# A new order of work in a fused attention and expert kernel: score pairs, half values and half down projections

## The chip, the cores and the metric

The kernel runs on one core of a Trainium2 chip. The metric is the device time of one launch in microseconds (us), lower is better; for the kernel before, three runs are given, and the median counts.

## The reference

The input is 64 sequences of 128 tokens and width 128, with a context of 120 tokens of width 96 for each. What is computed is one gated layer:

```
x = x + tanh(g_xattn) * cross_attention(layernorm(x), ctx)      # 16 heads of 8, biases, softmax over 120 keys
x = x + tanh(g_ffn)   * ffn_block(layernorm(x))
ffn_block(x):
    h = rms(x) ; q = rms(heads(h wq)) ; k = rms(heads(h wk)) ; v = heads(h wv)
    x = x + causal_softmax(q k / sqrt(8)) v wo                  # the first 32 columns of the product set to 0
    xf = rms(x) ; probs = softmax(xf gate) ; the best 2 of 4 experts, weights normalised
    moe = w0 gelu(xf up) down + w1 silu(xf w1)(xf w2) down + w2 four-layer gelu net + w3 three-layer gelu net
    return x + moe                                              # the first 32 columns of moe set to 0
```

All four experts are computed for every token, in fp32.

## The kernel before, in words

The 64 sequences are worked in 16 groups of 4. The work on a group is cut into five parts: N (layer norm of the input, transposes, the projections q, k, v of the cross attention), A (cross attention), B (norm and projections of the self attention), D (self attention, router, the first layers of the experts) and M (the later layers of the experts and the output). They are a software pipeline: in one step of the loop, part N works on group t+1, A on t, B on t-1, D on t-2 and M on t-3. Twelve steps form the loop (`LOOP`, t = 3 to 14); ahead of it stand four ramp steps (`first_group` to `fourth_group`) and behind it four tail steps, each with an order of its own (`RAMP`, `TAIL`; `last_queries`, t = 15, is made from the loop's order without N).

The order is written out by hand, as one list of uses for a step, `SCHEDULE = self_attention() + second_experts() + cross_attention() + first_experts()` (lines 112 to 160). Every engine walks through that list in its `step` function and issues its own part of each use, so one list sets the order on PE, ACT (ScalarE), DVE (VectorE), POOL (GpSimd) and SP's DMA queue alike. Engines run in order; a wait of one use holds all that stands behind it on that engine.

The eight PSUM banks belong to rings: four banks `w0` to `w3`, two banks `s2a`, `s2b` (the scores and, as ring "f", expert layers), one `pv` and one `t`. `bank_of_each_use` hands out the banks of a ring in turn, in the order of the list. A matmul waits until the former use of its bank has been read (`drained`), so the n-th use of the ring "w" waits for the reader of the use four places earlier.

The uses that the change and the prediction's steps touch:

- `exact(part, b, first)`: a pair of exact scores (s2), two fp32 matmuls of 512 columns for four heads each, into ps_s2a and ps_s2b (line 1342). ACT takes exponentials of each into `probs` (line 951). For D, POOL then masks both tiles of a pair in one select (lines 817 and 818), behind a tick.
- `values(part, b)`: four groups of eight small matmuls with `probs` (line 1363), into ps_pv; two batches share ps_pv, and the last of them is copied by ACT (oT, line 955). For D, each waits for the mask of its pair.
- `estimate(part, b)`: rough scores in bf16 for all 16 heads (lines 1302 and 1306) into all four w banks. DVE takes the negated maxima (line 1092), four reductions.
- mT: the transposed maxima (line 1315), copied by ACT and sent by SP's DMA into qd, on which the first exact scores of the next block wait. mH and mL are the same in halves, in the ramp.
- down e: the down projection of expert e, 16 matmuls (line 1389) into a w bank; DVE adds the four results into ym (line 1121).
- oT, nT, wo: transposes of the values (DVE: reciprocal line 1131, scaling line 1133), transposes back (ACT's copy, line 958) and the output projection (line 1376, DVE lines 1143 and 1148), all through the bank t.
- B: hT (transposes of hb, which DVE makes in line 1032), qk (line 1274, ACT's copy line 896), squares (POOL, line 829), sums (DVE, line 1067), root (ACT, line 905), scale (DVE, lines 1071 and 1073), qT and kT (transposes).
- B init: DVE writes x2 (line 1042). It waits for `xf_ready`, that is until ACT's `D norm` (four activations into xf, line 881) has read the old x2.
- D xfT: transposes of xf (line 1225) into a w bank; logits; then e1_w1, e1_w2, e2_l1, e3_down, e0_up, the first layers of the experts (line 1408).

In the loop's order the w ring is used like this (number of the use in the step): estimate A0 6 to 9, A1 10 to 13, down 0 14, A2 15 to 18; in the cross block v 27, down 2 28, xT 29, estimate B0 30 to 33, B1 34 to 37, down 3 38, xfT 39, B2 40 to 43, logits 44, e1_w1 45.

Of the kernel before, what the change touches and what calls it, by code (L numbers as in the profile page):

```python
# [31 lines left out]
P = 128  # L32
# [8 lines left out]
UP = P - KEEP  # L41
G = 4
# [4 lines left out]
NT = H // HT  # L47
VW = HD + 1
PACK = 2
# [42 lines left out]
def values(part, b):  # L92

    return [(part, "pv", (b, c), "pv" if b % 2 and c == NT - 1 else None) for c in range(NT)]
# [12 lines left out]
def down(e):  # L107

    return fill("M", "down", e, "w")
# [12 lines left out]


def second_experts():

    return (fill("M", "e2_l2", 0) + one("D", "wo", 0, "t") + one("B", "scale", 0, None) + fill("M", "e2_l2", 1)
            + estimate("A", 3) + values("D", 3) + fill("M", "e3_up", 0) + one("D", "oT", 1, "t") + fill("M", "e3_up", 1)
            + one("N", "stats", 0, None)
            + one("D", "nT", 1, "t") + one("A", "mT") + fill("M", "e2_l3", 0) + one("N", "norm", 0, None) + one("D", "wo", 1, "t")
            + one("D", "out", 0, None) + one("B", "qT") + one("B", "kT") + one("D", "squares", 0, None)  # L130
            + fill("M", "e2_l3", 1, "w"))
# [71 lines left out]
def fourth_group():  # L203
# [3 lines left out]
            + one("D", "wo", 0, "t") + estimate("A", 3) + values("D", 3) + one("D", "oT", 1, "t") + one("A", "mT")  # L207
            + one("B", "scale", 0, None) + one("D", "nT", 1, "t") + one("N", "stats", 0, None) + one("D", "wo", 1, "t")
# [16 lines left out]
def last_self_keys():  # L225
# [11 lines left out]
            + fill("M", "down", 2, "pv") + estimate("B", 2) + one("D", "norm", 2, None) + one("B", "init", 0, None) + one("B", "copy", 0, None)  # L237
            + one("D", "xfT", 0, "t") + fill("M", "down", 3, "pv") + one("M", "store", 0, None) + one("B", "v", 0, "f") + one("D", "logits", 0, "t")
# [22 lines left out]
def last_experts():  # L261

    return (fill("M", "down", 1, "t") + fill("M", "e2_l2", 0) + fill("M", "e2_l2", 1) + down(0) + fill("M", "e2_l3", 0) + fill("M", "e2_l3", 1)
            + fill("M", "e3_up", 0, "w") + fill("M", "e3_up", 1, "w") + down(2) + down(3) + one("M", "store", 0, None))
# [156 lines left out]
def build(nc, x, ctxT, weights, vcols, rows, out):  # L421
    ctx = ExitStack()
    with ctx:
# [782 lines left out]
        def _(pe):  # L1206
# [21 lines left out]
            def step(st):  # L1228
                for part, work, index in st.works:
# [149 lines left out]
                    elif work == "fill" and index[0] == "down":  # L1379
                        h = DOWN_OF[index[1]]  # L1380
                        if index[1] in (0, 1):
                            sources = st.settled(*(("f",) if st.parts == "M" and index[1] == 1 else ("w", "f")))
                        else:
                            sources = st.drains([("M", "fill", (h, k)) for k in range(2)])
                        for b, v in merged(sources, st.drains([], key)):
                            pe.wait_ge(drained[b], v)
                        for b in range(G):
# [70 lines left out]
```

## Time and profile before

| what | value |
|---|---|
| three runs | 1071.01, 1071.3, 1073.17 us; median 1071.3 |
| the profiled execution, its own time | 1074.17 us |
| span of the profiled execution | 1072.5 us |
| PE matmuls, busy | 1009.0 us, 94% of the span |
| VectorE, busy | 788.7 us, 74% |
| ScalarE, busy | 736.5 us, 69% |
| GpSimd, busy | 338.1 us, 32% |
| mean granted TensorE clock | 0.982 |
| chain of waits that ended last | PE 65%, DVE 14%, ACT 11%, issue 6%, DMA 2% |

The profiled execution is 1.7 us longer than its span, and 2.9 us above the median of the runs. The clock is given as a share of 2.4 GHz: 1.00 is 2.4 GHz and 0.50 is 1.2 GHz. PE's busy time counts matmuls whose ends are modelled, so two of them can overlap in the records; the distance between two starts is the surer reading of what work costs. An engine's idle time only matters where PE, or what PE waits for, stands behind it.

### The profile page before, as it was taken

The numbers are of one execution on the slowest core, as the hardware profiler recorded it, in microseconds if no ns is written. First come the engines' busy times: TensorE is split into PE (matmuls) and PEld (weight loads), VectorE is DVE, ScalarE is ACT, GpSimd is POOL, SyncE is SP. The second block draws the span as 40 slices with busy tenths as digits, with TensorE's granted clock in tenths as the row PEclk, the third lists the DMA queues.
The fourth block names the chain that finished last, engine by engine and source line by source line (L and its number), as shares of the span: only waits on it lengthen the run. The fifth ranks groups of instructions, "written<-read, shape, count | busy, mean of one in ns | idle before, by whom it ended". The sixth has DMA issues, their size and how long they took to land.

```text
span 1072.5 us, 26205 instructions
## 1 busy us (share of the span) xinstructions
PE 1009.0 (94%) x8649; PEld 627.7 (59%) x8649; DVE 788.7 (74%) x2172; ACT 736.5 (69%) x1334; POOL 338.1 (32%) x463
## 2 busy tenths in 40 slices
PE   6768799999999999999999999999999999999898
PEld 5445556556565655656565565656556565656565
DVE  8546878777877877787787778778777877774723
ACT  6465767676777767677776767777676777767453
POOL 5613424141422414142241414224141422404130
PEclk9868999999999999999999999999999999999999
DMA  7424432233342224334222443422244342221200
GB/s 233 127 72 158 133 104 89 88 130 128 115 134 96 87 88 130 128 115 135 97 86 88 130 128 115 135 96 87 88 130 128 115 135 96 82 79 49 83 1 20
DMA packets 77317, 114.28 MB, mean 107 GB/s; under 512 B 7776, under 2 KB 40160, under 8 KB 77152
## 3 DMA queue, kind: packets, MB, share of 16 engines
q1 hardware_dynamic: 76800, 111.53, 32.1%
q10 hardware_dynamic: 480, 2.26, 0.6%
q8 instruction: 23, 0.38, 0.1%
q14 instruction: 14, 0.11, 0.0%
HBM read 58.97 MB, written 53.74 MB: 105 GB/s over the span
## 4 chain that ended last, share of the span: by engine, by line
PE 65%; DVE 14%; ACT 11%; issue 6%; DMA 2%; SPq 1%; POOL 0%; ACTq 0%; DVEq 0%; POOLq 0%
PE ps_pv L1363 9%; PE ps_w L1389 9%; PE ps_s2a L1342 7%; PE ps_s2b L1342 5%; PE ps_s2a L1401 5%; PE ps_s2b L1408 4%; ACT probs L951 4%; PE ps_t L1225 4%; PE ps_w L1408 3%; PE ps_w L1274 3%; DVE mpadA L1092 3%; PE ps_t L1376 2%; PE ps_w L1225 2%; PE ps_w L1306 2%; PE ps_w L1302 2%
## 5 line engine op out<-in xcount | busy, mean ns | idle before, releaser
L951 ACT ACTIVATE probs<-ps_s2a 120x512 f32<-120x512 f32 (+1 forms) x256 | 153.4, 599 | 76.6 <-PE ps_s2a L1342 68.5
L1092 DVE TENSOR_REDUCE mpadB<-ps_w 128x4 f32<-128x512 f32 x240 | 148.8, 683 | 22.7 <-PE ps_w L1306 22.7
L1092 DVE TENSOR_REDUCE mpadA<-ps_w 128x4 f32<-128x480 f32 x224 | 131.5, 650 | 38.1 <-PE ps_w L1306 38.1
L951 ACT ACTIVATE probs<-ps_s2b 120x512 f32<-120x512 f32 (+1 forms) x256 | 153.5, 599 | 0.0
L818 POOL TENSOR_SCALAR_AFFINE_SELECT probs<-probs 128x1024 f32<-128x1024 f32 x128 | 139.8, 1092 | 0.0
L1389 PE MATMUL ps_w<-W,hid 128*128 128x96 f32 x976 | 121.3, 278 | 1.0 <-DVE split_k L985 0.9
L1389 PEld LDWEIGHTS ps_w<-W,hid 128*128 128x128 f32 x976 | 113.8, 192 | 10.4 <-issue 4.9
L786 POOL TENSOR_TENSOR rB<-vrB,neg_half 128x4 f32<-128x4 f32 x16 | 16.1, 1008 | 204.5 <-DVE veB L978 204.5
L1342 PE MATMUL ps_s2a<-qdA,kstA 128*120 128x512 f32 x128 | 70.2, 548 | 9.2 <-DMA qdA<-scratch_Aq 4.8
L1401 PE MATMUL ps_s2a<-hid,W 128*128 128x512 f32 x152 | 74.4, 604 | 0.0
L1121 DVE SCALAR_TENSOR_TENSOR ym<-ps_w,gates,ym 128x96 f32<-128x96 f32 x184 | 45.7, 311 | 38.6 <-PE ps_w L1389 38.6
L955 ACT ACTIVATE oT<-ps_pv 128x512 f32<-128x512 f32 x64 | 38.3, 598 | 50.9 <-PE ps_pv L1363 50.9
L1342 PE MATMUL ps_s2a<-qdB,kstB 128*128 128x512 f32 x128 | 64.6, 505 | 7.6 <-ACT probs L951 2.1
L1363 PE MATMUL ps_pv<-probs,VA 120*18 120x128 f32 x2048 | 71.2, 282 | 0.0
L947 ACT ACTIVATE hid<-ps_s2a 128x512 f32<-128x512 f32 x73 | 43.7, 599 | 40.0 <-PE ps_s2a L1401 30.9
L1363 PE MATMUL ps_pv<-probs,VB 128*18 128x128 f32 x2048 | 68.4, 274 | 0.0
L1363 PEld LDWEIGHTS ps_pv<-probs,VA 120*18 120x18 f32 x2048 | 51.9, 100 | 24.2 <-issue 22.9
L817 POOL TENSOR_TENSOR tick<-one 128x1 f32<-128x1 f32 x128 | 24.9, 194 | 117.5 <-ACT probs L951 113.2
L1363 PEld LDWEIGHTS ps_pv<-probs,VB 128*18 128x18 f32 x2048 | 50.5, 97 | 17.2 <-issue 16.9
L958 ACT ACTIVATE onT<-ps_t 128x256 f32<-128x256 f32 x64 | 24.5, 384 | 51.6 <-PE ps_t L1225 51.6
L1342 PE MATMUL ps_s2b<-qdA,kstA 128*120 128x512 f32 x128 | 59.3, 463 | 0.0
L825 POOL TENSOR_TENSOR ym<-yb,one 128x128 f32<-128x128 f32 x16 | 6.4, 398 | 166.2 <-DMA out_x<-ym 166.2
(279 smaller groups left out, 2170.3 us busy)
## 6 DMA issues: line engine op xcount, KB each, us to landing
scratch_Aq<-split_q SPq DMA_DIRECT2D x48, 256.0 KB, 2.4
qdA<-scratch_Aq SPq DMA_DIRECT2D x64, 192.0 KB
scratch_Bq<-split_q SPq DMA_DIRECT2D x48, 256.0 KB, 2.4
scratch_Bk<-split_k SPq DMA_DIRECT2D x48, 256.0 KB, 2.9
qdB<-scratch_Bq SPq DMA_DIRECT2D x64, 192.0 KB
kstB<-scratch_Bk SPq DMA_DIRECT2D x64, 192.0 KB
scratch_Ak<-split_k SPq DMA_DIRECT2D x48, 240.0 KB, 2.3
kstA<-scratch_Ak SPq DMA_DIRECT2D x64, 180.0 KB
```

Source lines behind the costliest of these rows:

```text
L818: pool.affine_select(out=tile, in_=tile, compare_op=ALU.is_ge, fill=0.0, base=0, pattern=[[0, 2 * HT], [1, P]], channel_multiplier=-1).the ...
L947: nc.scalar.activation(hid[:, HID_AT[index[0]] + index[1], :], bank[:], ACT.Gelu).then_inc(done, 1)
L951: nc.scalar.activation(probs[0:k, slot_of(part, *index), :], bank[0:k, :], ACT.Exp, scale=SCALE if part == "A" else 1.0).then_inc(done, 1)
L955: nc.scalar.activation(oT[:], bank[:], ACT.Copy).then_inc(done, 1)
L1092: nc.vector.tensor_reduce(pair[:, :, c, b % 2] if halves else mneg[p][:, :, c, b], bank[:, 0:HT * k].rearrange("p (h k) -> p h k", h=HT), ...
L1121: ins = nc.vector.scalar_tensor_tensor(out=ym[:, b, KEEP:P], in0=bank[:, b * UP:(b + 1) * UP], scalar=gates[:, b, e:e + 1], in1=y[:, b, KE ...
L1225: ins = nc.tensor.transpose(psum[st.bank[key]][:, b * P:(b + 1) * P], of(b), identf[:])
L1342: mm(o, kst[p][:, c, b * k:(b + 1) * k], qd[p][:, :, c, b * P:(b + 1) * P], start=True, stop=True).then_inc(done, 1)
L1363: ins = mm(psum[st.bank[last]][32 * j:32 * j + VS, at:at + P], VB[p][0:k, first:first + VS], probs[0:k, slot_of(part, b, c), j * P:(j + 1) ...
L1389: ins = mm(bank[:, b * UP:(b + 1) * UP], hid[:, HID_AT[h] + k, b * P:(b + 1) * P], w[f"down{index[1]}"][:, k * UP:(k + 1) * UP], start=k = ...
L1401: ins = mm(bank[:], w[name][:, k * HID + c * P:k * HID + (c + 1) * P], hid[:, HID_AT[h] + k, :], start=k == 0, stop=k == chunks[-1])
L1408: mm(bank[:], w[name][:, c * P:(c + 1) * P], xfT[:], start=True, stop=True).then_inc(done, 1)
```

## The change

The order of the loop's step and of two ramp steps is laid out anew; what is computed, and the number of matmuls, stay.

- `values` can be issued in halves (`early_values` for the first two groups of heads, `late_values` for the others).
- Down 0 and down 3 are issued in two halves in the loop's order: `head` (batches 0 and 1, no semaphore at its end) and `rest`, both into the same bank. The waits stand in the head. Where no other work stands between them (`down(e)`), the instructions are those of before.
- Self block: estimates no longer stand inside the two pairs of a batch. Between pairs stand halves of values, two qk, or a half of down 0. Estimates A1 and A2 move later (A2 into `second_experts`, with `scale` between A2 and A3), down 0 ahead of A1.
- `second_experts`: nT of the second pair of batches behind e2_l3 0; qT and kT ahead of wo 1, of D's out and of its squares.
- Cross block: down 3 moves from behind values A1 to behind xT, in halves; the output's store with it. Estimates B0, B1, B2 stand behind the second pair of batches 1, 2 and 3; D's norm and B's init now ahead of B0, and xfT behind A2's first pair.
- Third ramp step (t = 1): hT first, qk directly behind the first batch's pairs, mL behind them. Fourth ramp step: as the loop's self block.

In the new order the w ring's uses are: A0 6 to 9, down 0 10, A1 11 to 14, A2 15 to 18; v 27, down 2 28, xT 29, down 3 30, B0 31 to 34, xfT 35, B1 36 to 39, logits 40, B2 41 to 44, e1_w1 45.

```diff
+def early_values(part, b):
+    return values(part, b, 0, PACK)
+def late_values(part, b):
+    return values(part, b, PACK, NT)
...
 def self_attention():
-    return (one("N", "load", 0, None) + one("N", "ctx", 0, None) + exact("D", 0, 0) + one("B", "hT") + down(1) + exact("D", 0, 2)
-            + one("B", "qk", 0) + one("B", "qk", 1) + one("B", "qk", 2) + one("B", "qk", 3)
-            + exact("D", 1, 0) + estimate("A", 0) + exact("D", 1, 2)
-            + one("B", "squares", 0, None) + values("D", 0)
-            + exact("D", 2, 0) + estimate("A", 1) + exact("D", 2, 2)
-            + values("D", 1) + one("B", "sums", 0, None) + down(0)
-            + exact("D", 3, 0) + one("D", "oT", 0, "t") + estimate("A", 2) + exact("D", 3, 2)
-            + one("A", "base", 0, None) + values("D", 2) + one("D", "nT", 0, "t") + one("B", "root", 0, None))
+    return (one("N", "load", 0, None) + one("N", "ctx", 0, None) + exact("D", 0, 0) + one("B", "hT") + down(1)
+            + exact("D", 0, 2) + one("B", "qk", 0) + one("B", "qk", 1) + early_values("D", 0)
+            + exact("D", 1, 0) + one("B", "qk", 2) + one("B", "qk", 3) + late_values("D", 0)
+            + exact("D", 1, 2) + one("B", "squares", 0, None) + estimate("A", 0) + early_values("D", 1)
+            + exact("D", 2, 0) + head(0) + late_values("D", 1)
+            + exact("D", 2, 2) + one("B", "sums", 0, None) + rest(0) + one("D", "oT", 0, "t")
+            + exact("D", 3, 0) + early_values("D", 2) + estimate("A", 1) + one("D", "nT", 0, "t") + late_values("D", 2)
+            + exact("D", 3, 2) + one("A", "base", 0, None) + one("B", "root", 0, None))
 def second_experts():
...
+    return (one("D", "wo", 0, "t") + early_values("D", 3) + estimate("A", 2) + fill("M", "e2_l2", 0) + one("B", "scale", 0, None)
+            + late_values("D", 3) + fill("M", "e2_l2", 1) + estimate("A", 3) + fill("M", "e3_up", 0) + one("D", "oT", 1, "t")
+            + fill("M", "e3_up", 1) + one("N", "stats", 0, None) + one("A", "mT") + fill("M", "e2_l3", 0) + one("D", "nT", 1, "t")
+            + one("N", "norm", 0, None) + one("B", "qT") + one("B", "kT") + one("D", "wo", 1, "t")
+            + one("D", "out", 0, None) + one("D", "squares", 0, None) + fill("M", "e2_l3", 1, "w"))
 def cross_attention():
-    return (exact("A", 0, 0) + one("B", "v") + down(2) + exact("A", 0, 2) + one("N", "xT")
-            + exact("A", 1, 0) + estimate("B", 0) + exact("A", 1, 2)
-            + one("D", "norm", 0, None) + one("B", "init", 0, None) + one("B", "copy", 0, None) + values("A", 0)
-            + exact("A", 2, 0) + estimate("B", 1) + exact("A", 2, 2)
-            + values("A", 1) + down(3) + one("M", "store", 0, None) + one("D", "xfT")
-            + exact("A", 3, 0) + one("A", "oT", 0, "t") + estimate("B", 2) + exact("A", 3, 2)
-            + values("A", 2) + one("D", "logits") + one("A", "nT", 0, "t"))
+    return (exact("A", 0, 0) + one("B", "v") + down(2) + exact("A", 0, 2) + one("N", "xT") + head(3)
+            + exact("A", 1, 0) + rest(3) + one("M", "store", 0, None)
+            + exact("A", 1, 2) + values("A", 0) + one("D", "norm", 0, None) + one("B", "init", 0, None) + one("B", "copy", 0, None)
+            + estimate("B", 0)
+            + exact("A", 2, 0) + one("D", "xfT") + values("A", 1)
+            + exact("A", 2, 2) + one("A", "oT", 0, "t") + estimate("B", 1)
+            + exact("A", 3, 0) + values("A", 2) + one("D", "logits")
+            + exact("A", 3, 2) + estimate("B", 2) + one("A", "nT", 0, "t"))
...
 def third_group():
-    return (exact("A", 0, 0) + exact("A", 0, 2) + one("A", "mL", 0, "t") + exact("A", 1, 0) + values("A", 0) + one("B", "hT")
-            + exact("A", 1, 2) + one("B", "qk", 0) + one("B", "qk", 1) + one("B", "qk", 2) + one("B", "qk", 3)
-            + one("B", "squares", 0, None) + one("B", "copy", 0, None)
+    return (one("B", "hT") + exact("A", 0, 0) + exact("A", 0, 2)
+            + one("B", "qk", 0) + one("B", "qk", 1) + one("B", "qk", 2) + one("B", "qk", 3) + one("A", "mL", 0, "t")
+            + exact("A", 1, 0) + exact("A", 1, 2) + one("B", "squares", 0, None) + one("B", "copy", 0, None) + values("A", 0)
...
 def fourth_group():
-            + one("D", "wo", 0, "t") + estimate("A", 3) + values("D", 3) + one("D", "oT", 1, "t") + one("A", "mT")
-            + one("B", "scale", 0, None) + one("D", "nT", 1, "t") + one("N", "stats", 0, None) + one("D", "wo", 1, "t")
+            + one("D", "wo", 0, "t") + early_values("D", 3) + estimate("A", 2) + one("B", "scale", 0, None) + late_values("D", 3)
+            + one("D", "oT", 1, "t") + estimate("A", 3) + one("A", "mT") + one("D", "nT", 1, "t") + one("N", "stats", 0, None) + one("D", "wo", 1, "t")
```

## Rows read from the trace of the kernel before

**Rows 1.** Busy time by stretch, one loop step (528.15 to 590.70), the sum.
```profile
sum 62.55, PE 61.20 PEld 38.03 DVE 48.86 ACT 45.41 POOL 19.36; mean PE 15.30 PEld 9.51 DVE 12.21 ACT 11.35 POOL 4.84
```

**Rows 2.** Waits of PE's weight loads, one loop step: us in total, times, longest.
```profile
PEld ps_s2a L1342 <- ACT probs L951: 2.4, 6, 0.5
...
PEld ps_s2b L1342 <- ACT probs L951: 1.6, 6, 0.3
```

**Rows 3.** Timeline of PE, self block of a loop step: start us, us, instruction.
```profile
528.17 0.50 PE L1342 MATMUL ps_s2a<-qdB,kstB 128*128 128x512 f32 x1
...
541.55 0.48 PE L1342 MATMUL ps_s2a<-qdB,kstB 128*128 128x512 f32 x1
...
542.11 0.60 PE L1225 MATMUL ps_t<-identf,oT 128*128 128x128 f32 x4
...
543.02 0.38 PE L1306 MATMUL ps_w<-kdA,qTbA 32*128 32x480 bf16 x4 [0.32 <-DVE ym L1121]
```

**Rows 4.** Timeline of the same stretch, the other engines.
```profile
533.23 1.09 POOL L818 TENSOR_SCALAR_AFFINE_SELECT probs<-probs 128x1024 f32<-128x1024 f32 x1
...
537.84 1.89 POOL L829 TENSOR_TENSOR sq<-qk 128x1024 f32<-128x1024 f32 x1
...
539.98 1.21 DVE L1067 TENSOR_REDUCE hs<-sq 128x128 f32<-128x1024 f32 x1
...
541.88 0.99 DVE L1121 SCALAR_TENSOR_TENSOR ym<-ps_w,gates,ym 128x96 f32<-128x96 f32 x4 [0.69 <-PE ps_w L1389]
```

**Rows 5.** Timeline, the second experts of the same step.
```profile
547.88 0.94 DVE L1071 RECIPROCAL hr<-hr 128x128 f32<-128x128 f32 x1
...
548.86 1.23 DVE L1073 TENSOR_TENSOR qk<-qk,hr 128x1024 f32<-128x1024 f32 x1
...
550.00 2.35 DVE L1092 TENSOR_REDUCE mpadA<-ps_w 128x4 f32<-128x480 f32 x4
...
553.40 0.27 PE L1315 MATMUL ps_w<-identf,mpadA 128*128 128x128 f32 x1
```

**Rows 6.** Timeline, the cross block of the same step.
```profile
565.06 1.07 PE L1363 MATMUL ps_pv<-probs,VA 120*18 120x128 f32 x32
...
565.33 0.59 ACT L951 ACTIVATE probs<-ps_s2b 120x512 f32<-120x512 f32 x1
565.80 1.27 ACT L881 ACTIVATE xf<-x,rM 128x128 f32<-128x128 f32 x4
...
567.16 1.12 DVE L1042 TENSOR_SCALAR x<-x,mvB,rB 128x128 f32<-128x128 f32 x4 [0.30 <-issue]
...
568.20 2.48 DVE L1092 TENSOR_REDUCE mpadB<-ps_w 128x4 f32<-128x512 f32 x4
...
576.33 1.02 PE L1408 MATMUL ps_w<-xfT,W 128*128 128x512 f32 x2
```

**Rows 7.** Timeline, third ramp step.
```profile
53.22 1.11 DVE L1032 TENSOR_SCALAR hb<-x,mvB,rB 128x128 f32<-128x128 f32 x4 [1.13 <-POOL rB L786]
...
63.39 1.89 POOL L829 TENSOR_TENSOR sq<-qk 128x1024 f32<-128x1024 f32 x1 [9.22 <-ACT qk L896]
...
71.13 1.97 PE L1225 MATMUL ps_w<-identf,qk 128*128 128x128 f32 x8 [5.38 <-DVE qk L1073]
```

**Rows 8.** Fourth ramp step: timeline of PE, and the stretch 99.00 to 100.70.
```profile
93.41 0.48 PE L1342 MATMUL ps_s2a<-qdB,kstB 128*128 128x512 f32 x1
...
96.28 0.65 PE L1225 MATMUL ps_w<-identf,hb 128*128 128x128 f32 x4 [2.16 <-DVE hb L1032]
...
97.71 3.64 PE L1274 MATMUL ps_w<-W,hT 128*128 128x256 f32 x8 [0.31 <-ACT hT L893]
...
115.05 0.33 PE L1315 MATMUL ps_w<-identf,mpadA 128*128 128x128 f32 x1
...
124.83 0.63 PE L1225 MATMUL ps_w<-identf,xn 128*128 128x128 f32 x4 [1.72 <-DVE split_k L985]
...
99.00:100.70 1.70, 1.70 (x5) 1.35 (x4) 0.00 (x0) 0.76 (x3) 1.00 (x1) 0.50 1.01 360
```

More of the change, by code:

```diff
@@ L89, in estimate, with values @@
     return [(part, "s1", (b, c), rings[c]) for c in range(NT)]
-def values(part, b):
-    return [(part, "pv", (b, c), "pv" if b % 2 and c == NT - 1 else None) for c in range(NT)]
+def values(part, b, first=0, last=NT):
+    return [(part, "pv", (b, c), "pv" if b % 2 and c == NT - 1 else None) for c in range(first, last)]
+def early_values(part, b):
+    return values(part, b, 0, PACK)
+def late_values(part, b):
+    return values(part, b, PACK, NT)
 def one(part, work, index=0, ring="w"):
@@ L124, in second_experts @@
-def second_experts():
[L126 to L131, printed above, removed]
@@ L134, in cross_attention @@
-def cross_attention():
-    return (exact("A", 0, 0) + one("B", "v") + down(2) + exact("A", 0, 2) + one("N", "xT")
-            + exact("A", 1, 0) + estimate("B", 0) + exact("A", 1, 2)
-            + one("D", "norm", 0, None) + one("B", "init", 0, None) + one("B", "copy", 0, None) + values("A", 0)
-            + exact("A", 2, 0) + estimate("B", 1) + exact("A", 2, 2)
-            + values("A", 1) + down(3) + one("M", "store", 0, None) + one("D", "xfT")
-            + exact("A", 3, 0) + one("A", "oT", 0, "t") + estimate("B", 2) + exact("A", 3, 2)
-            + values("A", 2) + one("D", "logits") + one("A", "nT", 0, "t"))
+HEADED = (0, 3)
@@ new lines, in head, with rest, down @@
+def head(e):
+    return one("M", "head", e, None)
+def rest(e, ring="w"):
+    return fill("M", "down", e, ring)
+def down(e, ring="w"):
+    return (head(e) if e in HEADED else []) + rest(e, ring)
+def self_attention():
+    return (one("N", "load", 0, None) + one("N", "ctx", 0, None) + exact("D", 0, 0) + one("B", "hT") + down(1)
[6 more added lines that the diff above has]
+            + exact("D", 3, 2) + one("A", "base", 0, None) + one("B", "root", 0, None))
@@ L236, in last_self_keys @@
             + one("D", "squares", 2, None) + estimate("B", 1) + fill("M", "e2_l3", 1)
-            + fill("M", "down", 2, "pv") + estimate("B", 2) + one("D", "norm", 2, None) + one("B", "init", 0, None) + one("B", "copy", 0, None)
-            + one("D", "xfT", 0, "t") + fill("M", "down", 3, "pv") + one("M", "store", 0, None) + one("B", "v", 0, "f") + one("D", "logits", 0, "t")
+            + down(2, "pv") + estimate("B", 2) + one("D", "norm", 2, None) + one("B", "init", 0, None) + one("B", "copy", 0, None)
+            + one("D", "xfT", 0, "t") + down(3, "pv") + one("M", "store", 0, None) + one("B", "v", 0, "f") + one("D", "logits", 0, "t")
             + fill("D", "e1_w1", 0) + fill("D", "e1_w2", 0) + one("D", "keep", 0, None) + estimate("B", 3)
@@ L261, in last_experts @@
 def last_experts():
-    return (fill("M", "down", 1, "t") + fill("M", "e2_l2", 0) + fill("M", "e2_l2", 1) + down(0) + fill("M", "e2_l3", 0) + fill("M", "e2_l3", 1)
+    return (down(1, "t") + fill("M", "e2_l2", 0) + fill("M", "e2_l2", 1) + down(0) + fill("M", "e2_l3", 0) + fill("M", "e2_l3", 1)
             + fill("M", "e3_up", 0, "w") + fill("M", "e3_up", 1, "w") + down(2) + down(3) + one("M", "store", 0, None))
@@ L1378, in step @@
                         ins.then_inc(done, 1)
[L1379 to L1387, printed above, removed]
+                    elif work == "head" or work == "fill" and index[0] == "down":
+                        e = index if work == "head" else index[1]
+                        use, h = ("M", "fill", ("down", e)), DOWN_OF[e]
+                        if work == "head" or e not in HEADED:
+                            if e in (0, 1):
+                                sources = st.settled(*(("f",) if st.parts == "M" and e == 1 else ("w", "f")))
+                            else:
+                                sources = st.drains([("M", "fill", (h, k)) for k in range(2)])
+                            for b, v in merged(sources, st.drains([], use)):
+                                pe.wait_ge(drained[b], v)
+                        for b in range(0 if work == "head" or e not in HEADED else G // 2, G // 2 if work == "head" else G):
                             for k in range(2):
-                                ins = mm(bank[:, b * UP:(b + 1) * UP], hid[:, HID_AT[h] + k, b * P:(b + 1) * P],
-                                         w[f"down{index[1]}"][:, k * UP:(k + 1) * UP], start=k == 0, stop=k == 1)
-                        ins.then_inc(done, 1)
+                                ins = mm(psum[st.bank[use]][:, b * UP:(b + 1) * UP], hid[:, HID_AT[h] + k, b * P:(b + 1) * P],
+                                         w[f"down{e}"][:, k * UP:(k + 1) * UP], start=k == 0, stop=k == 1)
+                        if work == "fill":
+                            ins.then_inc(done, 1)
                     elif work == "fill" and index[0] in ("e2_l2", "e2_l3", "e3_up"):
```

2 lines of the change are left out of this document (removed).

## The prediction

> **What bounds it now.** I read the views in this order. First the table of the stretches of one loop step: in 62.55 us TensorE (PE) is busy 61.20, VectorE (DVE) 48.86, ScalarE (ACT) 45.41 and GpSimd (POOL) 19.36 [rows 1]. So PE's order of work sets the length of a step, and a gain is either less PE work or fewer stalls of PE. The matmuls of the change are the same before and after, so only stalls count. Then the waits of PE's weight loads in one step: the scores (s2) wait 2.4 us for the exponentials that free ps_s2a and 1.6 us for those that free ps_s2b [rows 2]. That is what the new order goes for. Then PE's timeline: one step begins at 528.17 and the next 62.54 us later; a pair of scores that waits for nothing takes 542.11 - 541.55 = 0.56 us before transposes and, by the same reading, about 0.65 before other work [rows 3]. Comparing every pair of a step with that, I find 1.4 us of stall in the self block (D) up to its last pair, and 1.55 in the cross block (A) up to the first e1_w1. These, 3 us in 62.5, are the most that plain pairs can win; the 4.0 us of waits counts some that lie under matmuls still running.
>
> Times below are us from the start of a step's first pair (528.17).
>
> **Self block.** Between pairs now stand half a set of values (0.5, half of the 1.0 between the starts of values and of the next pair, 565.06 and about 566.06 [rows 6]), half a down (about 0.9, half of the 1.8 us between the starts of a down and of the pair behind it), two qk, or an estimate. ACT takes exponentials 0.47 apart [rows 6], so 0.9 to 1.4 us of other work hides them: those stalls go. What comes instead are waits that two-pair spacing had hidden:
> - Values of a half need their mask. A mask lands 0.17 + 0.14 + 1.09 us after its second exponential, 1.40 in all (the select is the 1.09 [rows 4]). Early values of batch 1 reach PE at 7.9 and have it at 8.05: 0.15 of stall. The other halves come out 0 to 1 us clear.
> - POOL's squares (1.89), then DVE's sums (1.21), then down 0's four additions (0.99) are one chain [rows 4]. The squares stay behind batch 1's last mask, at 9.9, so they end at 11.8, the sums at 13.1, the additions at 14.05. Estimate A1 takes the bank of down 0 and stands only oT, one pair and half a set of values behind it: it reaches PE at 13.75 and starts at 14.2. Before, the same bank cost 0.32 [rows 3]. Behind it on DVE stand reciprocal and scaling of oT, so nT waits to 14.9: 0.35 more.
> Stalls in all 0.9 against 1.4: 0.5 gained at the end of the block.
> - Second experts: estimates A2 and A3 now both lie here, with DVE's scale between them. Its two steps take 0.94 and 1.23, 2.12 from start to start of the next group, and four maxima 2.35 [rows 5]. A2's maxima run 17.7 to 20.0, scale to 22.1, A3's to 24.4; PE is ready for mT at 24.1 and starts at 24.6. Before, mT was at 553.40 - 528.17 = 25.2 [rows 5]. That its DMA is then in front of the same work as before (qT, kT, e2_l3) costs nothing: 4.4 us lie between mT and the cross block, as before.
> I take the cross block as starting 0.4 us earlier (bounds: 1.4 earlier if none of these waits shows; 0.6 later if each is double).
>
> **Cross block.** Stalls on exponentials go here too. But norm of D now stands behind pair A1's second and *ahead* of all of estimate B0. On DVE init waits for ACT's four xf, and B0's maxima stand behind init. xfT, one pair after B0, takes the bank of B0's first maxima: on the ring of four it is the fourth use after it, where before three other uses lay between them in time. The chain from the last score of batch 1 (PE 36.5): exponential 37.15 to 37.75, xf from 0.47 after its start (565.80 - 565.33), 1.27 long, init 0.09 after its end, B0's maxima 1.04 after init's start (568.20 - 567.16), first maximum 0.68 of four in 2.48 [rows 6]. It ends at 40.7, and PE goes on at 40.8. PE itself has a score, values (1.0), B0 (0.54) and a pair till then and is there at 39.0: **1.8 us of stall in every step**, on a bank that the order of before kept free. From there DVE holds PE on: B1 has 2.48, logits, B2 2.48; e1_w1 needs B2's first maximum, 0.6 after PE is ready. Sum: stalls of cross 1.8 + 0.15 (oT) + 0.1 + 0.6 = 2.65 against 1.55. So e1_w1, at 576.33 - 528.17 = 48.16 before [rows 6], comes at 48.16 - 0.4 + 1.1 - 0.2 (the last for overlap of loads at the block's start) = 48.66. DVE's later work keeps this shift; its one spare wait (1.05, before oT's reciprocal) takes up the rest. Step: **+0.5 us**; 12 loop steps and the last queries' step, 13: +6.5. Bounds: -1.4 a step (no bank stall, only e1_w1's 0.6) to +1.5 (each new wait half as long again).
> Moving down 3 ahead of the estimates, in halves, costs nothing: its additions end at 37.8, as B0 (38.0) needs its bank, but there is no more room. The output's store goes with it, off the path. SP's queue keeps its order.
>
> **Ramp.** Third group: PE waits 5.38 us for DVE's scaled qk at 71.13, whose chain began when POOL could square at 63.39 [rows 7]. hb is ready at 54.3 (53.22 + 1.11), hT first; qk is then copied by 61.2, two us earlier. ACT's root stands behind pair A2's exponentials, so 1.85 us remain: **-1.85**. Only the first A pair waits, for hb, some 1.1 us, and PE has idle time behind it.
> Fourth group: without M's work nothing covers DVE. From its first pair (93.41) to mT are 21.6 us before (115.05 [rows 8]). After, A2 stands behind batch 3's pairs (at about 19.3; the masks alone hold PE 1.5 us), then DVE does 0.5 + 2.35 (A2) + 2.12 (scale) + 0.8 (oT) + 2.35 (A3) before mT: 27.4. qT and kT lie behind it, shorter afterwards by perhaps 0.5. With the cross stall, larger here by 1 because no rest of down 3 covers the exponentials: 5.8 - 0.5 + 2.1 = **+7.4** (bounds 0, if later waits shrink by as much, and +9).
> The two self-only tail groups and the last experts issue the same instructions as before.
>
> **Sum:** 6.5 - 1.85 + 7.4 = +12.0 us. The profiled execution took 1074.17 with a span of 1072.5; it would become 1086.2. Against the median of the runs, 1071.3, that is **1083.3**.
>
> **The clock.** A stall could also cost by TensorE's granted clock. After an idle 2.16 us (to 96.28) the clock was 0.50, the 1.2 GHz level, from 99.0 to 100.7, and four qk took 3.64 us in place of half as much; after an idle 1.72 us (to 124.83) no slow matmuls followed [rows 8]. The new stall of 1.8 lies between. I take nothing for it, since the loop around it is full, unlike both places, and keep the other end as a rival. The Trainium skill, "TensorE: Matmul & The Clock Gate", part "What's actually happening", has the clock fall only after an idle window as a whole; the place at 96.28, with matmuls before and behind it, speaks for a stricter chip. By the page the sum stays as it is.
>
> **Rivals.**
> 1. The bank of xfT is free in time (the page of waits shows no such stall now; if xf or init were sooner by 1.8). Then a step is 0.4 + 1.55 - 0.6 = 1.4 shorter: 13 x -1.4 = -18, with -1.85 and 5.5 in the ramp: **1057**, faster. For it: 4.0 us of waits on exponentials are real. Against: init's wait for xf is in the trace now (567.16 right behind 565.80 + 1.27). It decides as soon as the stall at xfT is under 0.9. Chance 0.2.
> 2. The clock falls after that stall: a slow stretch as at 97.71 costs 3.64 / 2 = 1.8 at most; in half of 13 steps +11: **1095**, in all 1107. Chance 0.15.
> 3. Masks: each of the halved values comes late by another 0.15 or so, since POOL's select waits for one pair alone; +1 a step: **1096**. Chance 0.1.
> 4. Gain and loss cancel: a step of -0.4. **1071**. Chance 0.07.
> The forecast has 0.48. Should the halves of down not really part (same matmuls, same instructions otherwise), nothing above changes, since its cover is counted only between pairs.
>
> **Numbers.** Forecast 1083.3, its own range 1073 to 1093. Over all cases I leave out the far ends of rivals 1 and 2: 1060 to 1099. Faster by over 0.2% 0.21, within 0.2% (what a measurement of this kernel can tell from none) 0.07, slower 0.72.
>
> **What would show it.** In the step after: waits of s2 on exponentials near zero; a wait of ps_w at the transposes of xf for DVE's mpadB of 1.5 to 2 us in every step, its weight load idle as long; DVE idle before init with xf on ACT as releaser; A1's estimate waiting for ym, nT for DVE's scaled oT, mT for mpadA about 0.5; step 63.0. Third group: PE's wait for qk about 3 to 4 us; fourth: mT some 27 us behind its first pair. Wrong it is if xfT starts right behind its pair, or a step is under 62.3.

## The result, and the profile after

The changed kernel takes **1104.76 us** (median of 4 runs, 1103.3 to 1107.81) against 1071.78 for the kernel before: a ratio of 1.0307, 95% interval 1.0289 to 1.0325. It is 33 us slower. The forecast was 1083.3 us, with 1060 to 1099 as its range: the right side, but a third of the size, and the result lies above the range.

The profiled execution has a span of 1102.5 us, against 1072.5. The records give PE the same busy time as before (1008.9 and 1009.0 us), and no matmul was added. Matmuls at the lower clock count as busy for longer, so these totals don't say how much of the 30 us is idling and how much is slower going; the steps below do. One loop step in four stretches, with its sum (columns: stretch, its length, then busy us and number of PE, PEld, DVE, ACT, POOL, the granted clock, DMA share, GB/s), which answers to [rows 1]:

```profile
542.18:558.79 16.61, 15.84 (x170) 11.12 (x171) 10.69 (x30) 12.03 (x24) 10.44 (x15) 1.00 0.51 172
558.79:572.90 14.11, 14.03 (x85) 7.13 (x84) 11.69 (x31) 10.25 (x17) 3.48 (x4) 1.00 0.11 34
572.90:591.90 19.00, 16.69 (x199) 11.96 (x197) 14.00 (x35) 14.20 (x27) 3.46 (x4) 1.00 0.54 179
591.90:606.37 14.47, 14.32 (x85) 7.22 (x85) 12.59 (x43) 8.91 (x17) 1.98 (x2) 1.00 0.04 15
sum 64.19, PE 60.88 PEld 37.43 DVE 48.96 ACT 45.39 POOL 19.36; mean PE 15.22 PEld 9.36 DVE 12.24 ACT 11.35 POOL 4.84
```

The step is 64.19 us long in place of 62.55, and the third stretch, the cross block, has 2.3 us in which PE does nothing. The waits of that step on PE (us in total, times, longest) answer to [rows 2]:

```profile
PE ps_w L1248 <- DVE mpadB L1115: 1.7, 1, 1.7
PE ps_w L1434 <- DVE mpadB L1115: 0.5, 1, 0.5
PE ps_w L1329 <- DVE ym L1144: 0.4, 1, 0.4
PE ps_t L1248 <- DVE on L1156: 0.2, 1, 0.2
```

and of its weight loads:

```profile
PEld ps_t L1248 <- DVE on L1156: 1.4, 2, 0.9
PEld ps_w L1338 <- DVE mpadA L1115: 0.9, 1, 0.9
PEld ps_s2a L1365 <- ACT hid L970: 0.9, 1, 0.9
PEld ps_pv L1386 <- POOL probs L841: 0.6, 2, 0.4
```

The 4.0 us of waits on exponentials are gone, as meant. The waits that the prediction named are there, and DVE has taken ACT's place as the engine that PE waits for. The large one, in the timeline (answers to [rows 6]; start us, us, engine):

```profile
580.48 1.27 ACT L904 ACTIVATE xf<-x,rM 128x128 f32<-128x128 f32 x4
...
581.84 1.11 DVE L1065 TENSOR_SCALAR x<-x,mvB,rB 128x128 f32<-128x128 f32 x4 [1.52 <-issue]
...
582.87 2.48 DVE L1115 TENSOR_REDUCE mpadB<-ps_w 128x4 f32<-128x512 f32 x4
583.70 0.63 PE L1248 MATMUL ps_w<-identf,xf 128*128 128x128 f32 x4 [1.72 <-DVE mpadB L1115]
```

The transposes of xf (583.70) start after 1.72 us of idling, when the first of B0's maxima (from 582.87) has been read out of their bank; the maxima stand behind init (581.84), init behind ACT's xf. DVE itself was idle for 1.52 us ahead of init. The view names no releaser for that ("issue"); what ties it to ACT is that init starts 0.09 us after the end of xf (580.48 + 1.27), as it did before [rows 6], and the first experiment.

The steps are not alike. From the transposes of hb in one step to the next I read 64.2 us in some and 65.3 to 65.5 in others, in turn from the fourth loop step on; before, the steps between the first and the last were all 62.55. In a long step the clock falls behind the idle time. Stretches of one such step, same columns as above:

```profile
516.50:518.20 1.70, 0.05 (x1) 0.00 (x0) 1.70 (x6) 0.94 (x2) 0.00 (x0) 1.00 0.70 186
518.30:521.50 3.20, 3.20 (x37) 2.24 (x38) 1.62 (x3) 0.97 (x2) 0.00 (x0) 0.50 0.52 173
522.00:525.00 3.00, 3.00 (x50) 1.83 (x49) 2.33 (x5) 2.07 (x4) 0.07 (x1) 1.00 0.00 0
```

After 1.7 us without matmuls the granted clock is 0.50 (1.2 GHz) from 518.3 to 521.5, then 1.00 again, and the step is 1.2 us longer. Six of the 13 steps (five of the loop and the last queries') have such a stretch. It costs 1.1 to 1.3 us each time, about 7.2 us in all.

From the transposes of hb in the first loop step to those behind the last queries' step are 841.2 us, against 813.0 before: 28.2 of the profiles' 30.0 us. Ahead of them lie 1.9 us: -2.9 up to DVE's hb at the end of the second ramp step, where nothing was changed, -3.0 from there to the first pair of the fourth ramp step, and +7.8 in that step.

In the fourth ramp step mT comes 114.64 - 87.50 = 27.1 us behind the step's first pair, in place of 21.6 [rows 8]:

```profile
87.50 0.47 PE L1365 MATMUL ps_s2a<-qdB,kstB 128*128 128x512 f32 x1
...
114.64 0.47 PE L1338 MATMUL ps_w<-identf,mpadA 128*128 128x128 f32 x1 [4.21 <-DVE mpadA L1115]
```

### The profile page after: what moved, and what is told of

Its sections match the earlier page's. It is cut to its first block, busy times and chain, and to the rows that moved or that the text cites. A ratio compares the mean times of both kernels' runs of the same rounds, so it can differ in the third digit from the quotient of the medians.

```text
span 1102.5 us, 26157 instructions
## 1 busy us (share of the span) xinstructions
PE 1008.9 (92%) x8649; PEld 622.1 (56%) x8649; DVE 790.1 (72%) x2172; ACT 736.8 (67%) x1334; POOL 338.3 (31%) x463
## 4 chain that ended last, share of the span: by engine, by line
PE 68%; DVE 13%; issue 8%; ACT 6%; POOL 3%; SPq 1%; DMA 1%; DVEq 0%; ACTq 0%; POOLq 0%
PE ps_pv L1386 10%; PE ps_w L1414 8%; PE ps_s2a L1365 7%; PE ps_s2a L1427 5%; PE ps_s2b L1434 4%; PE ps_s2b L1365 4%; PE ps_w L1248 4%; PE ps_w L1434 3%; PE ps_t L1248 3%; PE ps_s2b L1427 3%; PE ps_w L1297 3%; PE ps_w L1427 3%; PE ps_t L1399 3%; DVE mpadA L1115 2%; POOL sq L852 2%
## 5 line engine op out<-in xcount | busy, mean ns | idle before, releaser
L1414 PEld LDWEIGHTS ps_w<-W,hid 128*128 128x128 f32 x976 | 118.0, 192 | 9.8 <-issue 4.5
L1386 PE MATMUL ps_pv<-probs,VB 128*18 128x128 f32 x2048 | 79.9, 277 | 2.1 <-POOL probs L841 2.0
L1386 PE MATMUL ps_pv<-probs,VA 120*18 120x128 f32 x2048 | 73.9, 289 | 0.0
L978 ACT ACTIVATE oT<-ps_pv 128x512 f32<-128x512 f32 x64 | 38.2, 597 | 47.9 <-PE ps_pv L1386 47.9
L1386 PEld LDWEIGHTS ps_pv<-probs,VB 128*18 128x18 f32 x2048 | 46.0, 97 | 37.8 <-issue 23.5
L1154 DVE RECIPROCAL rden<-ps_t 128x32 f32<-128x32 f32 x63 | 22.2, 353 | 52.5 <-PE ps_t L1248 52.5
L1434 PE MATMUL ps_w<-xfT,W 128*128 128x512 f32 x104 | 53.2, 603 | 7.0 <-DVE mpadB L1115 7.0
L970 ACT ACTIVATE hid<-ps_s2b 128x512 f32<-128x512 f32 x60 | 35.8, 597 | 30.2 <-PE ps_s2b L1427 26.1
```

Source lines behind the costliest of these rows:

```text
L970: nc.scalar.activation(hid[:, HID_AT[index[0]] + index[1], :], bank[:], ACT.Gelu).then_inc(done, 1)
L978: nc.scalar.activation(oT[:], bank[:], ACT.Copy).then_inc(done, 1)
L1386: ins = mm(psum[st.bank[last]][32 * j:32 * j + VS, at:at + P], VB[p][0:k, first:first + VS], probs[0:k, slot_of(part, b, c), j * P:(j + 1) ...
L1414: ins = mm(psum[st.bank[use]][:, b * UP:(b + 1) * UP], hid[:, HID_AT[h] + k, b * P:(b + 1) * P], w[f"down{e}"][:, k * UP:(k + 1) * UP], st ...
L1434: mm(bank[:], w[name][:, c * P:(c + 1) * P], xfT[:], start=True, stop=True).then_inc(done, 1)
```

## The experiments

"Theory T" is that of this study once the result was known: 1.64 us a step from the new order, more for the clock, and the fourth ramp step. "The mended kernel" is that of the first experiment, e1. Each "+" and "-" in a cut of code is against the changed kernel, or the version named; "..." stands for lines left out.

**Maxima ahead of init.** PE's order stays; on DVE, estimate B0's maxima come before init. An estimate has work on PE and DVE alone, and norm, init and copy have none on PE, so DVE's order is the only one that changes.

```diff
-            + exact("A", 1, 2) + values("A", 0) + one("D", "norm", 0, None) + one("B", "init", 0, None) + one("B", "copy", 0, None)
-            + estimate("B", 0)
+            + exact("A", 1, 2) + values("A", 0) + estimate("B", 0)
+            + one("D", "norm", 0, None) + one("B", "init", 0, None) + one("B", "copy", 0, None)
```

> The changed kernel with one edit: estimate B0 stands ahead of D's norm, B's init and B's copy in the cross block (in the loop and wherever that list is used). PE's order is the same; on DVE B0's maxima come before init. Theory T (the 1.72 us wait of the transposes of xf is DVE's order: init waits for ACT's xf and B0's maxima stand behind it): that wait goes to 0 to 0.2 us, e1_w1's 0.50 stays or shrinks, no slow clock in the loop; a step of 62.3 to 62.7, total 1074 to 1082. Rival R1 (the wait is DVE's load, and only moves on): it reappears at estimate B1 or e1_w1 with 1 us or more, a step stays over 63.5, total 1092 or more.

Measured: 1077.03 us, 1.0051 times the kernel before (1.0033 to 1.0070). All inner loop steps are 62.68 us, and none has a slow stretch. The timeline:

```profile
568.77 1.27 ACT L904 ACTIVATE xf<-x,rM 128x128 f32<-128x128 f32 x4
569.64 2.49 DVE L1115 TENSOR_REDUCE mpadB<-ps_w 128x4 f32<-128x512 f32 x4 [1.04 <-PE ps_w L1329]
...
570.49 0.63 PE L1248 MATMUL ps_w<-identf,xf 128*128 128x128 f32 x4 [0.21 <-DVE mpadB L1115]
...
572.05 1.11 DVE L1065 TENSOR_SCALAR x<-x,mvB,rB 128x128 f32<-128x128 f32 x4
```

The maxima (569.64) now run beside xf, init comes after them, and the wait is 0.21. e1_w1's 0.50 stays. One exchange on DVE is worth 27.7 us: 1.5 us in each of 13 steps (19.6), and about 7.2 for the clock; the rest, under 1 us, lies outside these steps or in the spread of the runs.

**The idle time filled.** Ten matmuls into the free bank ps_t, ahead of the wait for xf; results unused.

```diff
+                        if st.parts == PARTS:
+                            for b, v in st.drains([], ("A", "oT", 0)):
+                                pe.wait_ge(drained[b], v)
+                            keep_busy(10)
                         pe.wait_ge(xf_ready, g + 1)
```

> The changed kernel, with ten idle-filling matmuls of 128 columns into the free bank ps_t ahead of the wait for xfT, in the loop's steps only (about 1.1 us of PE work inside the 1.72 us of idling; results unused). Theory T (every second step pays 1.2 us because the idling lets the granted clock fall): the slow stretches of the loop go, all steps take 64.2, total 1104.8 - 6 x 1.25 = 1097. Rival R2 (the slow stretches hide under DVE, and the 1.2 us come from elsewhere): total 1104 to 1106, steps still alternate.

Measured: 1101.89 us (1.0277, 1.0247 to 1.0307). The filling was longer than I had thought, 2.2 us in place of 1.1, a little over the idle time (the trace has two records for each of the ten fp32 matmuls):

```profile
514.98 2.39 PE L1235 MATMUL ps_t<-identf 128*128 128x128 f32 x20
517.21 0.60 PE L1248 MATMUL ps_w<-identf,xf 128*128 128x128 f32 x4
```

So each step is 64.47 us, 0.28 over the short steps of the changed kernel; but they are all alike, and the loop has no slow stretch any more. More matmuls, less time: 0.28 x 12 paid, the clock's share saved. That every long step was the clock's doing is shown by the steps. The total misses the 1097 that was forecast: the median is 3 us lower, where 7.2 - 3.4 = 3.8 are worked out, and the runs of the two kernels just touch (1098.6 to 1103.5 against 1103.3 to 1107.8), so the total alone would show little.

**Cross block alone.** Self block, second experts, third and fourth ramp step as before.

```diff
 def self_attention():
-            + exact("D", 0, 2) + one("B", "qk", 0) + one("B", "qk", 1) + early_values("D", 0)
+            + one("B", "qk", 0) + one("B", "qk", 1) + one("B", "qk", 2) + one("B", "qk", 3)
...
```

> The cross block new, the self block, second experts, third and fourth ramp step as before. Theory T (the cross block costs 1.15 us in each of 13 steps, plus about 1.2 in every second one for the clock): 1071.8 + 15 + 8 = 1095, range 1088 to 1100; xfT's wait is 1.7 in every step. Rival R3 (the two blocks only cost together, since the late maxima of A push DVE's later work): xfT's wait under 1 us, total under 1083.

Measured: 1102.2 us (1.0274, 1.0245 to 1.0304), over my range. xfT's wait is 1.72 in each loop step. A step without a slow stretch is 63.8 us (+1.25, near what was meant), but of the 11 steps behind the first only two are so: nine are 65.0 to 65.1, and the last queries' step has a slow stretch too. 13 x 1.25 + 10 x 1.2 = 28 us, of the 30 measured. The same stall costs the clock in nearly all steps here and in every second one of the changed kernel. What differs is the length of a step, 65.0 against 64.2 and 65.4, so where in time the stall falls. I did not vary that by itself, so why one kernel pays more often than the other is not shown; that the penalty can't be carried over from one version to the next is.

**Cross block undone.** The changed kernel with the cross block of before.

```diff
 def cross_attention():
-    return (exact("A", 0, 0) + one("B", "v") + down(2) + exact("A", 0, 2) + one("N", "xT") + head(3)
-            + exact("A", 1, 0) + rest(3) + one("M", "store", 0, None)
+    return (exact("A", 0, 0) + one("B", "v") + down(2) + exact("A", 0, 2) + one("N", "xT")
+            + exact("A", 1, 0) + estimate("B", 0) + exact("A", 1, 2)
...
```

> The changed kernel with the cross block as before (down 3 in one piece there). Theory T (the self block costs 0.5 us a step by seams between half values and by mT, the ramp 1 to 2): steps of 63.0, no slow clock in the loop, total 1071.8 + 13 x 0.5 + 1 = 1079, range 1075 to 1083. Rival R4 (the self block gains as first forecast, 0.4 a step): steps of 62.1, total 1066 to 1070.

Measured: 1079.59 us (1.0071, 1.0047 to 1.0096); steps of 63.07 to 63.14, +0.55, no slow stretch. So the self block loses too, and the parts add up for a step: 0.55 + 1.25 is 1.8, against 1.64 for both. That the total fell inside the range is partly luck. The forecast had 1 us for the ramp; in the profile the fourth ramp step is 6.3 us longer than before (62.45 against 56.13 between transposes of hb), and the time ahead of it 7.7 us shorter (88.63 against 96.28), 3.0 of that up to hb, where nothing was changed.

**Fourth ramp step as before**, on the mended kernel (its self block and what follows up to the cross block).

```diff
-    return (one("D", "mL", 0, "t") + of_parts("NABD", self_attention())
-            + one("D", "wo", 0, "t") + early_values("D", 3) + estimate("A", 2) + one("B", "scale", 0, None) + late_values("D", 3)
-            + one("D", "oT", 1, "t") + estimate("A", 3) + one("A", "mT") + one("D", "nT", 1, "t")
+    return (one("D", "mL", 0, "t") + of_parts("NABD", self_attention_before())
+            + one("D", "wo", 0, "t") + estimate("A", 3) + values("D", 3) + one("D", "oT", 1, "t") + one("A", "mT")
+            + one("B", "scale", 0, None) + one("D", "nT", 1, "t")
...
```

> e1_maxima_first, with the fourth ramp step's own part laid out as before (its self block and what follows up to the cross block); the loop stays new. Theory T (the fourth step pays 5.5 us, since mT waits 4.2 us for DVE's maxima behind A2, scale and oT): mT 21.6 us behind the step's first pair, not 27.2; total 1077.0 - 5.5 = 1071.5, range 1069 to 1074. Rival R5 (later waits had taken that up): total 1075 or more.

Measured: 1074.15 us (1.0025, 1.0000 to 1.0051). mT, without a wait, at 109.44, against a first pair at 87.83: 21.6 us.

```profile
109.44 0.33 PE L1350 MATMUL ps_w<-identf,mpadA 128*128 128x128 f32 x1
```

From the transposes of hb in the fourth step to those in the next are 57.3 us, 5.4 less than in the first experiment (62.7). The medians differ by 2.9 only, where 5.5 was forecast, and 1074.15 lies just above the range of 1069 to 1074; the runs of this kernel spread from 1070 to 1077. The wait is shown, its worth in the total only roughly.

**The mended cross block with the self block of before**, and with the new third ramp step.

```diff
 def second_experts():
-    return (one("D", "wo", 0, "t") + early_values("D", 3) + estimate("A", 2) + fill("M", "e2_l2", 0) + one("B", "scale", 0, None)
+    return (fill("M", "e2_l2", 0) + one("D", "wo", 0, "t") + one("B", "scale", 0, None) + fill("M", "e2_l2", 1)
...
```

> The cross block of e1_maxima_first and the new third ramp step, with the self block, second experts and fourth ramp step of before. Theory T (the self block costs 0.53 a step, the mended cross block gains): steps of 62.68 - 0.53 = 62.15, total 1077.0 - 13 x 0.53 - 5.5 = 1064.6, range 1062 to 1067, so faster than the kernel before by 0.6%. Rival R6 (before's self block hands A's and B's DVE work over later, so that the mended cross block does not gain on it): steps of 62.5 or more, total 1069 or more.

Measured: **1068.27 us**, 0.9977 times the kernel before (0.9960 to 0.9994). Steps are 62.31 us: the cross block with plain pairs gains 0.24 us a step, once its DVE order is right. That is a little over half of the 0.40 that I had worked out (62.15), and the total lies between T's range (to 1067) and R6's (from 1069). It is the first version whose median is below that of the kernel before, by 0.2%.

**Whole values.** D's values as one set, at the place of the late half.

```diff
-            + exact("D", 0, 2) + one("B", "qk", 0) + one("B", "qk", 1) + early_values("D", 0)
-            + exact("D", 1, 0) + one("B", "qk", 2) + one("B", "qk", 3) + late_values("D", 0)
+            + exact("D", 0, 2) + one("B", "qk", 0) + one("B", "qk", 1)
+            + exact("D", 1, 0) + one("B", "qk", 2) + one("B", "qk", 3) + values("D", 0)
...
```

> e1_maxima_first with the values of D whole, at the place of the late halves, in the self block and the second experts (the fourth step's own last pair stays halved). Theory T (a half set of values takes 0.56 us where half of a whole one takes 0.50, and a change to values behind qk or a down costs 0.1 to 0.2 more): 0.5 us of halves and 0.2 of the change behind qk go, 0.2 to 0.4 of waits of scores on exponentials come back; steps 62.2 to 62.6, total 1071 to 1076. Rival R7 (the halves cost nothing, they are only cover): scores wait more, steps 62.9 or more, total 1080 or more.

Measured: 1077.41 us (1.0066, 1.0046 to 1.0086), the same as with halves; steps 62.80, 0.12 longer, between T's 62.2 to 62.6 and R7's 62.9. Each theory holds in part. Added up from the starts on PE up to the last layer ahead of the cross block (us of one step, from the start of each group to the start of the next):

| group | before | changed | mended (e1) | mended, whole values |
|---|---|---|---|---|
| eight pairs of D's scores | 6.00 | 4.94 | 4.93 | 6.10 |
| D's values | 4.00 | 4.99 | 4.97 | 4.00 |
| four qk | 1.53 | 1.91 | 1.92 | 1.64 |
| e2 and e3 layers | 7.42 | 7.70 | 7.69 | 7.69 |
| all up to the last e2_l3 | 28.36 | 28.85 | 28.86 | 28.97 |

One wait hides in these rows. A1's estimate waits for its bank (ym), and the table counts that to the group ahead of it, here in the changed kernel:

```profile
555.62 0.63 PE L1386 MATMUL ps_pv<-probs,VB 128*18 128x128 f32 x16
556.68 0.38 PE L1329 MATMUL ps_w<-kdA,qTbA 32*128 32x480 bf16 x4 [0.42 <-DVE ym L1144]
```

That half set has 1.06 us from start to start, where the other seven have 0.56. With whole values it is a pair that has 1.28 there in place of 0.65. With the wait (0.50 and about 0.6) taken out, halves cost 4.49 - 4.00 = 0.49 us, and pairs without halves between them wait not 1.17 but about 0.55 more.

So plain pairs give back 1.06 us of waits. The halves take 0.49 of it, two pairs of qk 0.38, and the e2 and e3 layers, which now have values or an estimate as neighbours, 0.28: 1.15 in all. What two qk cost depends on what stands behind them, as one step of the version with whole values has it, 0.68 us ahead of a pair and 0.96 ahead of values:

```profile
532.05 1.03 PE L1297 MATMUL ps_w<-W,hT 128*128 128x256 f32 x4
532.73 0.58 PE L1365 MATMUL ps_s2a<-qdB,kstB 128*128 128x512 f32 x1
...
533.49 1.02 PE L1297 MATMUL ps_w<-W,hT 128*128 128x256 f32 x4
534.45 1.07 PE L1386 MATMUL ps_pv<-probs,VB 128*18 128x128 f32 x32
```

**Third ramp step as before**, on the mended kernel.

```diff
-    return (one("B", "hT") + exact("A", 0, 0) + exact("A", 0, 2)
+    return (exact("A", 0, 0) + exact("A", 0, 2) + one("A", "mL", 0, "t") + exact("A", 1, 0) + values("A", 0) + one("B", "hT")
...
```

> e1_maxima_first with the third ramp step as before. Theory T (hT and qk first start POOL's and DVE's chain to the scaled qk earlier): PE's wait for the scaled qk 5.4 us, not 2.5; total 1077.0 + 2.5, range 1078 to 1081. Rival R8 (the third step's gain is only where the clock's slow stretches fell): total 1076 to 1078.

Measured: 1078.83 us (1.0065, 1.0047 to 1.0083). PE's wait for the scaled qk is 5.39 us again, 2.47 in the new order. But from DVE's hb to the first pair of the fourth step are 37.3 us, with the order of before, and 35.3 to 37.7 in nine profiles of the new one; the kernel before and the cross block alone had 40.2 and 38.2. The means lie 2 us apart and overlap, and the totals are 1.8 apart inside their intervals. The gain in the wait is shown, its worth in time is not settled.

**B2's maxima earlier**, on the 1068.27 us version: estimate B2 ahead of the block's last pair.

```diff
-            + exact("A", 3, 0) + values("A", 2) + one("D", "logits")
-            + exact("A", 3, 2) + estimate("B", 2) + one("A", "nT", 0, "t"))
+            + exact("A", 3, 0) + values("A", 2) + one("D", "logits") + estimate("B", 2)
+            + exact("A", 3, 2) + one("A", "nT", 0, "t"))
```

> e6_cross_mended_self_before, with estimate B2 ahead of the last pair of scores of the cross block (directly behind logits), so that its maxima begin some 0.6 us earlier. Theory T (the 0.50 us wait of e1_w1 is for B2's first maximum, which stands one pair too near): that wait goes, steps of 61.8 to 62.0, total 1068.3 - 13 x 0.4 = 1063, range 1061 to 1065. Rival R9 (B2 then waits as long for DVE's reading of the logits, its bank): steps stay at 62.2 to 62.4, total 1067 to 1070.

Measured: 1068.24 us (0.9966, 0.9951 to 0.9981), steps 62.35. A miss for T, and what R9 said: e1_w1's wait of 0.50 is gone, and 0.4 comes back in front of B2, for DVE's reading of the logits.

```profile
PE ps_w L1326 <- DVE lg L1106: 0.4, 1, 0.4
PE ps_w L1330 <- DVE ym L1145: 0.3, 1, 0.3
PE ps_w L1249 <- DVE mpadB L1116: 0.2, 1, 0.2
```

**Scale behind A3's maxima**, on the mended kernel.

```diff
-    return (one("D", "wo", 0, "t") + early_values("D", 3) + estimate("A", 2) + fill("M", "e2_l2", 0) + one("B", "scale", 0, None)
-            + late_values("D", 3) + fill("M", "e2_l2", 1) + estimate("A", 3) + fill("M", "e3_up", 0) + one("D", "oT", 1, "t")
+    return (one("D", "wo", 0, "t") + early_values("D", 3) + estimate("A", 2) + fill("M", "e2_l2", 0)
+            + late_values("D", 3) + fill("M", "e2_l2", 1) + estimate("A", 3) + one("B", "scale", 0, None) + fill("M", "e3_up", 0) + one("D", "oT", 1, "t")
...
```

> e1_maxima_first with DVE's scale behind the maxima of A3, in the loop and in the fourth ramp step, instead of between A2's and A3's. Theory T (mT waits for A3's maxima behind scale: 0.9 us of idle weight loads in the loop, 4.2 us in the fourth step): both waits go or shrink to 0.2 and 2.1; steps 62.3 to 62.5, total 1077.0 - 13 x 0.3 - 2 = 1071, range 1069 to 1074. Rival R10 (qT then waits for the scaled qk as long): steps of 62.6 or more, total 1075 or more.

Measured: 1086.44 us (1.0132, 1.0111 to 1.0153), steps of 63.5: slower than the mended kernel by 9 us, and T is wrong here. R10's numbers hold, though not its wait: it is not qT that waits for the scaled qk. mT still waits 0.9; the waits of PE's weight loads in a step:

```profile
PEld ps_t L1248 <- DVE on L1156: 2.9, 3, 1.5
PEld ps_w L1338 <- DVE mpadA L1115: 0.9, 1, 0.9
```

In the changed kernel DVE had done scale and was idle for 0.23 us ahead of A3's maxima, so scale did not hold them up:

```profile
565.00 2.35 DVE L1115 TENSOR_REDUCE mpadA<-ps_w 128x4 f32<-128x480 f32 x4 [0.23 <-PE ps_w L1329]
...
567.41 0.33 PE L1338 MATMUL ps_w<-identf,mpadA 128*128 128x128 f32 x1
```

So mT waits because four maxima take 2.35 us and only two layers and oT stand between A3 and mT; scale was not in it. Moved behind A3, scale delays oT's reciprocal and scaling, for which nT's loads now wait 1.5 us at the longest, where it was 0.9. In the fourth step, where scale did stand in the chain, mT's wait fell from 4.21 to 2.86.

## Why the prediction was wrong

The sum was 12.0 us; 33 were measured. Two terms failed: the self block, forecast as 0.4 us a step won and measured as 0.49 lost, because divided and rearranged groups of matmuls were given no price of their own; and the clock, taken at nothing, which cost about 7.2 us. Its steps, in its order:

- **What bounds the kernel:** right that PE's order of work sets the step, and waits on exponentials went to none. "so only stalls count" was not: the same matmuls in another order took longer from start to start, without a wait (self block).
- **The mechanism at xfT:** right to 0.1 us: "1.8 us of stall in every step" was 1.72, e1_w1's 0.6 was 0.50. The first experiment shows the cause: DVE's order, init ahead of B0's maxima.
- **Self block:** wrong by 0.9 us a step. "The cross block as starting 0.4 us earlier" was 0.49 later (28.85 against 28.36 for the start of the last e2_l3). The waits named are there: A1's estimate 0.42 and nT 0.25, where I had 0.45 and 0.35; the masks hold weight loads for 0.6 but no half set starts more than 0.1 late by them (I had 0.15). The stalls won back were 1.06, where I had read 1.4. The term that failed is "half a set of values (0.5, half of the 1.0 ...)": I costed a divided group at half of a whole one, and a change of work at nothing. By the section on whole values that is 0.49 for halves, 0.38 for qk and 0.28 for the layers, 1.15 us a step, more than the whole miss. In the timeline of PE:

```profile
545.90 1.03 PE L1297 MATMUL ps_w<-W,hT 128*128 128x256 f32 x4
546.86 0.63 PE L1386 MATMUL ps_pv<-probs,VB 128*18 128x128 f32 x16
547.42 0.50 PE L1365 MATMUL ps_s2a<-qdB,kstB 128*128 128x512 f32 x1
...
550.49 0.63 PE L1386 MATMUL ps_pv<-probs,VB 128*18 128x128 f32 x16
551.05 0.50 PE L1365 MATMUL ps_s2a<-qdB,kstB 128*128 128x512 f32 x1
```

and in that of the kernel before:

```profile
535.64 1.07 PE L1363 MATMUL ps_pv<-probs,VB 128*18 128x128 f32 x32
536.64 0.50 PE L1342 MATMUL ps_s2a<-qdB,kstB 128*128 128x512 f32 x1
```

A whole set takes 1.00 from start to start, half a one 0.56 without any wait, and two qk 0.96 with values behind them, where half of the four took 0.77 (1.53 / 2). No mask is waited for there: POOL has the masks of the two halves behind qk done at 546.56 and 548.35, and they start at 546.86 and 548.94.

- **Cross block:** near. From the last e2_l3 to the next step are 35.34 us against 34.19, +1.15, where I had 0.9.
- Together 1.64 us a step where the forecast had 0.5: 13 x 1.14 = 15 of the 21 us that were missing.
- **The clock:** "I take nothing for it, since the loop around it is full" was wrong; a full loop around the stall is no protection. Rival 2 named the mechanism and priced it at 11 us for half of the steps, 1.8 each; six steps had it, at 1.1 to 1.3 each, about 7.2 us. The first two experiments show it. There had been two places to judge by, 2.16 us idle with a slow stretch behind and 1.72 idle without; the same 1.72 us was followed by a slow stretch in some steps here and by none in others. The Trainium skill, "TensorE: Matmul & The Clock Gate", part "What's actually happening", has the clock fall only after an idle window as a whole. By that rule, as I had read it, the clock would have cost nothing here. The trace disagrees: the slow stretch at 518.3 has only 1.72 us without matmuls ahead of it, and matmuls on both sides.
- **Third ramp step:** -1.85 in the forecast. The wait for the scaled qk fell by more, from 5.38 to 2.46, and the means of the profiles are 2 us apart. Their spread is as large, so what the step gained is not settled.
- **Fourth ramp step:** right: mT at 27.1 (forecast 27.4), and 7.8 us more from its transposes of hb to those of the next step (7.4). The stall at xfT is there too, 1.55 us; behind mT this step takes 39.66 us, and 37.16 with the cross block undone, against 37.36 before.
- **The chances:** rivals 2 and 3 were priced one at a time on top of a forecast without them. Cases that don't shut each other out add up, and an upper end with both had been 1083 + 11 + 13 = 1107. That the measured time lies near this sum is luck: rival 2 came at 7.2 us and not 11, and the late masks of rival 3 did not come; the place of its 13 us is taken by the price of halves and of changes of work, which no rival named.

## What to carry to other kernels

When work is put in front of a wait, look on *every* in-order engine at what else the list has moved: here one line of order on DVE, with PE's order unchanged, was worth 28 of 33 us. A divided group of small matmuls is not two halves; take the price of a change of work from the timeline (0.06 to 0.28 us here) times the number of changes, and set it against the waits that it hides. And a regular stall in a full PE (1.72 us here) can have a second price, the clock's, which came in some steps and not in others: measure it by filling the stall, or by taking the stall away.

## What the runs showed of the hardware that I had not expected

- The same 1.72 us of idling was followed by a slow stretch in nearly all steps of one kernel, in every second one of another. Filled with idle matmuls, no step had a slow stretch, and the median was 3 us lower, though each step issues 0.28 us more than fits.
- The start varies: DVE's hb of the second ramp step begins at 50.2 to 54.6 us in the twelve profiles, though nothing ahead of it was changed. In this part two single profiles can't show a difference of 2 us.
- A set of 32 small matmuls with its loads takes 1.00 us from start to start, two sets of 16 take 0.56 each. The group ahead of them pays too: two qk take 0.96 ahead of values and 0.68 ahead of a pair, the first e2_l2 1.92 ahead of values and 1.72 ahead of wo.
